# Sliding-window attention through a scratch in DRAM: rows of the scratch reordered by part, q or k, element and head, with the head interleave moved from the DMAs to the copies

## What is computed

```python
def _sliding_window_attention(q, k, v, w):          # w = 128, 16 heads of 16 elements
    ...
    scores = jnp.einsum('bhcid,bhcjd->bhcij', q_c, k_c)
    scores = jnp.where(valid[None, None], scores, big_neg)
    probs = jax.nn.softmax(scores, axis=-1)
    out = jnp.einsum('bhcij,bhcjd->bhcid', probs, v_c)
...
x = x + jnp.tanh(g_xattn[0]) * _L0_xattn_ref(_layernorm(x, axis=-1), ctx_1024, ctx_1024)
```

## Time and profile before

| | |
|---|---|
| median of 3 runs | 730.18 us (728.52 to 731.24) |
| the profiled execution | 729.61 us, its span 727.9 us |
| PE busy | 678.6 us, 93% |
| VectorE, GpSimd, ScalarE busy | 51%, 46%, 43% |
| mean DMA rate | 174 GB/s |
| attention | from the start to about 190 us |
| DMA issues of the scratch | 48 writes of 128 KB, 96 reads of 64, 128 and 192 KB |

### The profile page before, as it was taken

One profiled execution on the slowest core, in us unless ns is written; L12 is line 12 of the kernel. 1 busy time (PEld: TensorE's weight loads), 2 busy tenths in 40 slices (PEclk: granted clock), 3 DMA queues, 4 the chain that ended last, 5 costly groups with the idle time before them and its releaser, 6 DMA issues.

```text
span 727.9 us, 16246 instructions
## 1 busy us (share of the span) xinstructions
PE 678.6 (93%) x5228; PEld 545.5 (75%) x5234; DVE 367.7 (51%) x1131; ACT 315.2 (43%) x843; POOL 336.5 (46%) x504
## 2 busy tenths in 40 slices
PE   4889999999999999998999879999998999999995
PEld 2447777776758999997766534899896899789974
DVE  3568888998566645452788778112113121312220
ACT  3436666656554433332678651423232333232321
POOL 6334333332016655433458871644545455455423
PEclk9999999999999999999999999999999999999998
DMA  6995666671958999942344464679995658355521
GB/s 207 182 199 115 132 128 131 132 122 20 301 179 288 380 371 376 372 132 67 82 80 63 78 211 156 191 205 306 311 266 126 166 119 241 68 155 102 146 32 15
DMA packets 153143, 126.57 MB, mean 174 GB/s; under 512 B 51266, under 2 KB 142701, under 8 KB 153067
## 3 DMA queue, kind: packets, MB, share of 16 engines
q1 hardware_dynamic: 143258, 113.02, 55.6%
q0 software_dynamic: 9808, 12.60, 8.3%
HBM read 163.24 MB, written 23.87 MB: 257 GB/s over the span
## 4 chain that ended last, share of the span: by engine, by line
PE 68%; DVE 11%; SPq 6%; DMA 6%; issue 4%; ACT 3%; POOL 2%; DVEq 0%; ACTq 0%; POOLq 0%
PE e_HP L1278 12%; PE e_Y L1316 11%; PE e_HP L1020 8%; PE e_Y L1032 8%; PE O L671 4%; PE S L641 3%; PE S L659 3%; PE S L1927 2%; DVE a_nm L523 2%; SPq L2532 2%; DMA c_flat<-c_att 2%; PE e_HP L1927 2%; PE e_Y L1330 1%; PE S L661 1%; PE S L643 1%
## 5 line engine op out<-in xcount | busy, mean ns | idle before, releaser
L1361 ACT ACTIVATE w_down<-e_HP,e_col 128x128 f32<-128x128 f32 x256 | 73.1, 369 | 142.6 <-PE e_HP L1278 142.0
L1278 PEld LDWEIGHTS e_HP<-e_rT,w_up 128*128 128x128 f32 x1024 | 118.6, 192 | 5.3 <-issue 3.1
L1278 PE MATMUL e_HP<-e_rT,w_up 128*128 128x128 f32 x1024 | 120.3, 276 | 1.7 <-DVE e_rT L1383 0.9
L1316 PE MATMUL e_Y<-w_down 128*128 128x256 f32 x512 | 115.6, 379 | 0.0
L1459 POOL DMA_INDIRECT out<-e_yo,d_table x38 | 61.1, 1608 | 117.3 <-DVE e_yo L1415 75.5
L1316 PEld LDWEIGHTS e_Y<-w_down 128*128 128x128 f32 x512 | 94.9, 190 | 11.6
L1412 DVE TENSOR_TENSOR e_yo<-e_Y,e_b2b 128x256 f32<-128x256 f32 x35 | 14.8, 424 | 165.0 <-PE e_Y L1316 144.4
L523 DVE TENSOR_REDUCE a_nm<-S 128x2 f32<-128x512 f32 x128 | 83.0, 682 | 22.7 <-PE S L643 22.6
L379 ACT ACTIVATE a_pexp<-S 128x1024 f32<-128x1024 f32 x64 | 64.8, 1015 | 26.2 <-PE S L661 26.0
L1065 ACT ACTIVATE e_hT<-e_HP,e_col 128x128 f32<-128x128 f32 x128 | 36.5, 370 | 58.2 <-PE e_HP L1020 55.0
L1020 PEld LDWEIGHTS e_HP<-e_rT,w_up 128*128 128x128 f32 x512 | 59.5, 192 | 2.2 <-DVE e_rT L1078 1.5
(11 more groups left out here) (405 smaller groups left out, 1263.1 us busy)
## 6 DMA issues: line engine op xcount, KB each, us to landing
w_up<-L_ffn_w_in SPq DMA_DIRECT2D x38, 1024.0 KB
w_down<-L_ffn_w_in SPq DMA_DIRECT2D x32, 1024.0 KB
w_up<-L_ffn_W_in SPq DMA_DIRECT2D x16, 1024.0 KB, 9.3
w_down<-L_ffn_W_in SPq DMA_DIRECT2D x16, 1024.0 KB, 11.5
scr<-a_parts SPq DMA_DIRECT2D x48, 128.0 KB
e_b2b<-L_ffn_b_in SPq DMA_DIRECT2D x48, 128.0 KB, 4.1
x_sb<-L_ffn_w_in SPq DMA_DIRECT2D x6, 1024.0 KB
ctx_sb<-L_ffn_w_in SPq DMA_DIRECT2D x6, 1024.0 KB
```

The lines of the kernel that those rows point to most:

```text
L1278: m = e.matmul(HP[i % 2][:, j, :], w1[:, s, k, P * j:P * j + P], rT[:, r, k, :], start=(k == 0), stop=(k == 1))
L1316: m = e.matmul(Y[r][:, 0:D], hT[:, r, j, :], w2[:, s, j, :], start=(j == 0), stop=(j == NJ - 1))
L1361: m = e.activation(hT[:, r, j, :], HP[i % 2][:, j, :], ACT.Gelu, bias=col[:, n % 4, j:j + 1])
```

## The change

The scratch gets the order part, q or k, element, head, token. One DMA writes a unit, in runs of 256 tokens (512 bytes), from 128 partitions in the order (element, head). Each read takes whole rows (head, token) of 2,048 elements, 4,096 bytes. To have the partitions in the order (element, head), ScalarE and GpSimd turn the 128 columns in `normalise` and `copy_ctx`: their output stays contiguous, and their input is read in steps of 16 elements. The semaphore counts follow (16 a write in place of 48).

```diff
-        scr = nc.dram_tensor("scr", [4, 3, DH, HU, 2, S], BF16, kind="Internal").ap()
+        scr = nc.dram_tensor("scr", [4, 3, 2, DH, HU, S], BF16, kind="Internal").ap()
@@ write_parts
-                for f in range(3):
-                    e.dma_start(scr[u.mod(4), f].rearrange("d h s t -> h d (s t)"),
-                                parts[:, u.mod(2), 2 * f:2 * f + 2, :].rearrange("p s t -> p (s t)")).then_inc(s_scw[u.mod(2)], 16)
+                e.dma_start(scr[u.mod(4)].rearrange("f s d h t -> (d h) (f s) t"), parts[:, u.mod(2)]).then_inc(s_scw[u.mod(2)], 16)
@@ read_heads
-                cnt = 48 * (u.c // 2 + 1) if u.reg is None else u.reg * 96 + 48 * (u.c // 2 + 1)
+                cnt = 16 * (u.c // 2 + 1) if u.reg is None else u.reg * 32 + 16 * (u.c // 2 + 1)
                 for r0, f0, nf in ((0, 0, 3), (3 * DH, 1, 2), (5 * DH, 2, 1)):
                     for s, dst in ((0, q6), (1, k6)):
                         ff = (0, 3 - f0) if s == 0 else (f0, 3)
-                        e.dma_start(dst[r0:r0 + DH * nf, u.mod(4), :, :],
-                                    scr[u.mod(4), ff[0]:ff[1], :, :, s, :].rearrange("f d h t -> (f d) h t")
+                        e.dma_start(dst[r0:r0 + DH * nf, u.mod(4), :, :].rearrange("p h t -> p (h t)"),
+                                    scr[u.mod(4), ff[0]:ff[1], s].rearrange("f d h t -> f d (h t)")
@@ copy_ctx
-                e.tensor_copy(cu[:, n.mod(2), :, :], ctx_sb[:, bass.ds(n.tile(), 2), P * n.mod(2):P * n.mod(2) + P]
-                              ).then_inc(s_cu, 1)
+                e.tensor_copy(cu[:, n.mod(2), :, :].rearrange("p c (d h) -> p c d h", d=DH),
+                              ctx_sb[:, bass.ds(n.tile(), 2), P * n.mod(2):P * n.mod(2) + P].rearrange(
+                                  "p c (h d) -> p c d h", d=DH)).then_inc(s_cu, 1)
@@ normalise
-                    e.activation(qn[:, n.mod(2), c:c + 1, :], x_sb[:, bass.ds(t, 1), P * n.mod(2):P * n.mod(2) + P],
-                                 ACT.Identity, bias=nmr[:, bass.ds(t, 1)], scale=rstd[:, bass.ds(t, 1)]).then_inc(s_qn, 1)
+                    e.activation(qn[:, n.mod(2), c:c + 1, :].rearrange("p c (d h) -> p c d h", d=DH),
+                                 x_sb[:, bass.ds(t, 1), P * n.mod(2):P * n.mod(2) + P].rearrange(
+                                     "p c (h d) -> p c d h", d=DH), ACT.Identity, bias=nmr[:, bass.ds(t, 1)], scale=rstd[:, bass.ds(t, 1)]).then_inc(s_qn, 1)
@@ first_parts
-                    cnt = 48 * (v.c // 2 + 1) if v.reg is None else v.reg * 96 + 48 * (v.c // 2 + 1)
+                    cnt = 16 * (v.c // 2 + 1) if v.reg is None else v.reg * 32 + 16 * (v.c // 2 + 1)
```

## The result

The changed kernel takes 800.5 us, median of 6 runs (798.24 to 806.8), against 729.6 us for the kernel before in the same comparison (6 runs): a ratio of 1.0964, 95% interval 1.0929 to 1.0999. The forecast was 800 us, range 770 to 842, and slower by over half a per cent with a chance of 87%. The profiled execution took 802.86 us, its span 801.2.

What follows compares the result with a forecast made beforehand. TensorE bounds the 9.20 us step before; afterwards the first DMA engine was to, at 13.25 us a unit (reads 10.6, write 2.35, maxima 0.3). Sum +69.8 us on 729.61, forecast 800 us, range 770 to 842.

Steps and rivals of the forecast that it cites:

- The mechanism: Scratch DMAs: a transfer is dealt out over its outermost dimension; write on 16 engines, reads on 3, 2 and 16.
- both rivals that left the time at 727 to 730: Reads spread over all 16 engines, 727 us; or few engines but others each time, 730; they share 10%.
- The path that sets the end: Attention, from read 0 through the first engine's queue to unit 15's first pass: 168.57 moves to 238.4, +69.8 us.
- the first wait for `a_mts`: Sign in the opening: TensorE's first wait for the copied maxima becomes about 20 us longer.
- what follows: Everything after unit 15's first pass: unchanged and moved as a whole, by the sum of +69.8 us.
- The row of 4,096 bytes: Reads: a row priced at 25.5 GB/s for a busy engine, 0.16 us; 66 rows, 10.6 us a unit.
- The write's run of 512 bytes: Scratch write: 0.048 us a run, 48 runs to an engine, 2.35 us a write (1.2 to 4.7).
- From there the engine never runs empty: First engine from unit 4's reads on: each read finds the one before still running; 154.0 us, to 236.9.
- Dear writes: Rival on the scratch write: 512-byte runs cost double towards DRAM, 14 writes of 2.35 us more, 835 us; 5%.
- The clock: Rival on TensorE: clock stays low after waits, a step's 9.2 us may take 15, 28 us more, 827; 12%.
- What was costed at nothing: Turned copies on ScalarE (two instructions, 0.87 us together) and GpSimd (0.39, perhaps 0.58 us): hidden.
- 0.16 us against 8 x 0.048: Reads: on one engine, a 4,096-byte row against eight 512-byte runs, given as favouring long rows.

Runs made afterwards that it cites:

- the run with 80 matmuls: Changed kernel with 80 short matmuls on TensorE, results overwritten, ahead of the wait for the reads of every second unit: 802.96 us, ratio 1.0961.
- the kernel with cut three-part reads: Changed kernel with each read of three parts cut into three reads of one part, two-part reads kept: 771.28 us, ratio 1.0528.
- three kernels: Changed kernel with one-part reads (0.9954); changed kernel with part and element joined in the scratch (0.9968); kernel before with the turned copies and 128-outermost writes (0.9964).
- the kernel with joined parts: Changed kernel with q or k ahead of the part in the scratch, so part and element join to 48, 32 or 16 outermost: 729.08 us, ratio 0.9968.

## Why the prediction was right, point by point

**The mechanism held, and is shown.** The reads ran on 3 and 2 engines (0.18 and 0.13), the write on all (0.97); with all engines under the reads the kernel is back at 728.4 and 729.08 us. The stretches with old writes alone told it beforehand, and both rivals that left the time at 727 to 730 are excluded.

**The path that sets the end held nearly to the microsecond.** Forecast and measured: maxima of unit 0 landed at 72.6, second pass at 73.09; reads of unit 4 issued at 81.4, at 82.48; first pass of unit 15 at 238.4, at 238.75. One sign failed: the first wait for `a_mts` was to be about 20 us longer and is 4.5 longer, 6.00 for 1.51, because TensorE had already waited 10.88 us behind VectorE and the late `x`. And what follows does not quite move as a whole: the span is 73.3 us longer where the first pass of unit 15 came 70.2 later. The other 3 us arise behind the first mixture of experts, whose last matmul of L1020 starts 70.1 us later; in the second mixture the first matmul of L1278 starts 71.8 us later and the last 73.4. Why was not looked into.

**The terms are less good than their sum.**
- The row of 4,096 bytes: 0.16 forecast, 0.16 measured where two engines work. But beside reads on all engines it costs 0.25, which the prediction did not have.
- The write's run of 512 bytes: taken as 0.048 us, because runs seemed to cost by number; measured 0.026, the low bound, 27 ns by bytes. A write costs each engine 1.3 us and not 2.35.
- "From there the engine never runs empty": not so. The reads issued at 162.09 found the queue all but empty; in the last stretch shown below nothing moves at all. From 135.03 to 162.09 are 27.1 us for two units, whose rows and writes by the measured prices are 2 x (66 x 0.16 + 1.3 + 0.3) = 24.3. Some 2.8 us a pair are left for gaps and dearer rows; with the clock kept up two units take 25.7 us, so up to half of the 2.8 comes with the slow step.

Stretches of the changed kernel, the end of a pair's transfers and the gap before the next data:

```profile
160.90:162.90 2.00, 2.00 (x26) 1.82 (x24) 1.80 (x5) 1.00 (x2) 0.23 (x2) 1.00 0.65 201
163.00:163.60 0.60, 0.60 (x10) 0.35 (x11) 0.60 (x2) 0.60 (x2) 0.28 (x2) 1.00 0.00 0
```

One error made a unit 1.1 us too dear, the other 1.1 to 1.4 too cheap: 13.25 was forecast, 13.2 measured, and part of the precision is luck. So is the agreement of two mechanisms: by load alone a pair is 24.3 to 25.7 us, by issue to landing plus slow step 14.9 + 12.2 = 27.1, and 26.5 was forecast.

**Dear writes.** This rival was priced at 835; 14 writes of 2.35 us more on 799.4 are 832. At 0.026 us a run it falls in either case.

**The clock.** The rival had the mechanism: the clock falls behind the wait, the step takes longer, and the next reads are issued only after it. It had the size wrong, 12.1 us where 15 was feared. It also had its worth wrong: in the changed kernel shorter steps gained only 0.4 us a unit in the run with 80 matmuls, since the queue of the first two engines then sets nearly the same pace. It counts in full as soon as the queue is relieved.

**What was costed at nothing** cost nothing: the turned copies, dearer by a fifth on ScalarE and by over a half on GpSimd, are hidden in the run that has them with the old reads.

**Left open.** How the 12.1 us from issue to landing in the kernel with cut three-part reads divide into load and latency; and whether the 0.3 to 0.5% that three kernels gain over the one before come from the opening alone. The traces fit it: the kernel with joined parts reaches unit 0's second pass 2.9 us earlier and the attention's last one 3.4 us earlier, the other two 1.3 and then 1.7 to 1.9 us. No run separates it, and the kernel before itself had medians of 729.6, 731.35 and 732.31 us in the three comparisons, as far apart as the gain.

## What to carry to other kernels

Before a DMA's view is rearranged, look at what stands outermost on both sides afterwards: here the order chosen for long rows left 3 and 2 outermost, which made a transfer five to eight times poorer in engines, and a reordering of the scratch by one place brought it back. A stretch in which only one kind of transfer is in flight tells, by its DMA share, how many engines that kind gets. When a transfer must land within one step, both its load on the busiest engine and the time from first issue to last landing have to fit, and a wait of TensorE costs once more if its clock falls and the step behind is on the path.

## What the runs showed that was not expected

Long rows hardly speed up reads that use all engines. With joined parts the reads alone move 173 GB/s at a share of 0.85, 12.7 GB/s for a busy engine; the old reads in 512-byte runs moved 166 at 0.98. Two engines alone reach 25.5 each with the same rows. So the prediction's comparison for one engine, 0.16 us against 8 x 0.048, set rows on idle engines beside runs on crowded ones. What limits the 16 together, near 170 GB/s, no run here tells.

SyncE issues the simpler reads faster, 0.42 us in the kernel with joined parts against 0.60 before. And where the first engines have much queued, an issue takes longer: the copy of the maxima at 57.78 held SyncE for 5.30 us in the changed kernel, 0.83 in the one before. That the issue waits for room on those engines is inferred, not shown.
